# A GNN layer's node stage: another order of ScalarE's and TensorE's work within a step

## What is computed

```
h        = relu(layernorm(x))                             # every node
em       = relu(LN([h[src], h[dst]] @ msg_w + msg_b)) * edge_weight
messages = segment_mean(em, dst)                          # zero for a node without edges
gate     = sigmoid(h @ gate_w + gate_b)
h_new    = relu(LN([h, messages] @ upd_w + upd_b))
out      = x + gate * h_new + (1 - gate) * h
```

## Time and profile before

| | |
|---|---|
| median of 3 runs | 932.8 us |
| span of the profiled execution, first to last instruction | 994.9 us |
| granted TensorE clock, 100 to 500 us (node stage) | 0.50 |
| VectorE, ScalarE, TensorE busy over the span | 90%, 89%, 72% |
| mean granted TensorE clock over the span | 0.695 |

### The profile page before, as it was taken

How to read it: one execution, slowest core, us unless ns; L and a number is a source line. 1 busy time by engine, 2 the same in 40 slices (tenths; PEclk the granted TensorE clock), 3 DMA queues, 4 the chain that set the end, 5 groups by cost and what they waited for, 6 DMA issues and landing times.

```text
span 994.9 us, 19018 instructions
## 1 busy us (share of the span) xinstructions
PE 711.9 (72%) x3696; PEld 556.2 (56%) x3696; DVE 896.4 (90%) x3914; ACT 881.3 (89%) x3758; POOL 672.5 (68%) x602
## 2 busy tenths in 40 slices
PE   2477778777777777777756767787778787777861
PEld 1355556555555555555545656666656666666651
DVE  7499999999999999999997489999989999999984
ACT  3499999998999899989987689999999999999973
POOL 4677878777666667677757357677666776665466
PEclk9655555555555555555567789899889889998995
DMA  4244544455545555555423112233311211111110
GB/s 142 54 125 157 160 145 156 152 164 155 159 153 166 156 157 156 164 158 156 135 75 93 45 56 92 80 95 97 97 63 53 66 64 65 61 54 57 53 70 33
DMA packets 60147, 107.94 MB, mean 108 GB/s; under 512 B 14278, under 2 KB 16150, under 8 KB 60082
## 3 DMA queue, kind: packets, MB, share of 16 engines
q1 hardware_dynamic: 39756, 71.88, 20.8%
q0 software_dynamic: 18912, 34.84, 13.5%
q10 hardware_dynamic: 1414, 0.53, 0.2%
HBM read 56.01 MB, written 55.12 MB: 112 GB/s over the span
## 4 chain that ended last, share of the span: by engine, by line
ACT 60%; PE 13%; issue 11%; DVE 6%; another core or an unknown queue 6%; POOL 3%; ACTq 1%; DMA 1%; DVEq 0%; POOLq 0%
ACT hrow L392 16%; ACT junk L399 16%; ACT work L426 10%; ACT xload L392 4%; PE pt L1177 3%; ACT rs L379 3%; PE pm L1229 3%; ACT lnv L374 3%; POOL out L596 3%; PE pm L1231 3%; ACT work L1102 2%; PE py L1248 2%; ACT at L1045 2%; ACT work L1045 2%
## 5 line engine op out<-in xcount | busy, mean ns | idle before, releaser
L596 POOL DMA_INDIRECT out<-work,sidx x196 | 209.4, 1069 | 124.4 <-issue 55.6
L591 POOL DMA_INDIRECT ring<-in_x,src_i x196 | 220.0, 1123 | 90.5 <-issue 57.3
L1177 PE MATMUL pt<-ident,hrow 128*128 128x128 f32 x588 | 147.4, 399 | 142.6 <-ACT hrow L392 119.5
L426 ACT ACTIVATE work<-work,gt 128x128 f32<-128x128 f32 x589 | 205.1, 426 | 4.2 <-issue 3.0
L1211 PE MATMUL py<-w_u,work 128*128 128x129 f32 x784 | 204.5, 442 | 0.0
L1211 PEld LDWEIGHTS py<-w_u,work 128*128 128x128 f32 x784 | 175.6, 329 | 40.8 <-issue 40.8
L1177 PEld LDWEIGHTS pt<-ident,hrow 128*128 128x128 f32 x588 | 99.0, 202 | 175.6 <-ACT hrow L392 146.0
L591 POOL DMA_INDIRECT ring<-in_x,gidx x140 | 156.9, 1121 | 53.7 <-issue 42.2
L399 ACT ACTIVATE junk<-py 128x128 bf16<-128x128 f32 x588 | 155.4, 293 | 29.9 <-remote 29.8
L392 ACT ACTIVATE hrow<-xload,nb,rs 128x128 f32<-128x128 f32 x392 | 163.5, 514 | 3.0 <-DVE nb L385 2.7
L458 DVE SCALAR_TENSOR_TENSOR work<-py,rs,g_upd 128x128 f32<-128x128 f32 x588 | 163.2, 338 | 0.0
(11 more groups left out here) (163 smaller groups left out, 1506.7 us busy)
## 6 DMA issues: line engine op xcount, KB each, us to landing
xload<-in_x SPq DMA_DIRECT2D x98, 256.0 KB
out<-work SPq DMA_DIRECT2D x98, 256.0 KB
running_sums<-acc SPq DMA_DIRECT2D x49, 256.0 KB
staged_target_rows<-work SPq DMA_DIRECT2D x14, 256.0 KB
ring<-staged_target_rows SPq DMA_DIRECT2D x14, 256.0 KB
ring<-in_x,src_i POOLq DMA_INDIRECT x196
out<-work,sidx POOLq DMA_INDIRECT x196
ring<-in_x,gidx POOLq DMA_INDIRECT x140
```

The source lines that it names most:

```text
L426: last = nc.scalar.activation(t_buf[:, g.at % 4, k, :], t_buf[:, g.at % 4, k, :], ACT.Relu, scale=gt[:, g.at % 4, k:k + 1])
L591: pool.indirect_dma_start(out=dest, out_offset=None, in_=rows, in_offset=bass.IndirectOffsetOnAxis(ap=idx, axis=0), **(if_tail if rows is ...
L596: pool.indirect_dma_start(out=out, out_offset=bass.IndirectOffsetOnAxis(ap=idx, axis=0), in_=rows, in_offset=None, **if_tail).then_inc(s, 16)
L1177: last = nc.tensor.transpose(dest[:, k * H:(k + 1) * H], rows[:, k, :], ident[:, :])
```

## The change

ScalarE's step becomes: one gated row, logarithm, second gated row, reciprocal deviation, two gated rows, evacuation, four squares, gate exponential, four normalised rows. The special order of the first four steps goes. TensorE's step becomes: bias and product of group s-2, then the flip of group s-1. No instruction, wait, buffer or size is added or removed; a few register instructions of the loops aside, the same instructions stand in another order. The last six node steps run inside `edge_step`, whose ScalarE order stays, while TensorE's `node_step` is called there too and has the new order.

```diff
@@ ScalarE, node_step(s), after logs(act, nd, s, 2 * G)
-                filling = not beyond(s, 4)
-                if filling:
-                    rstds(act, nd, s, 2 * G)
+                if live(r, NG):
+                    gated_relu(act, nd, r, 2, first=1, done=False)
+                rstds(act, nd, s, 2 * G)
+                if live(r, NG):
+                    gated_relu(act, nd, r, first=2)
                 g = s.back(2)
                 if live(g, NG):
                     evacuate(nd, g, ht_dst[:, g.at % 4, :], pt[:, g.at % 2, :], ACT.Copy, "ht", "flip")
-                if not filling:
-                    rstds(act, nd, s, 2 * G)
-                if live(r, NG):
-                    gated_relu(act, nd, r, first=1)
+                node_post(s)
                 node_h(s)
-                node_post(s)
@@ TensorE, node_step(s)
-                g = s.back(1)
-                if live(g, NG):
-                    nd["h"].after(pe, g)
-                    one_mark(nd["flip"], pe, g, flip(pt[:, g.at % 2, :], hrow[:, g.at % 4]))
                 g = s.back(2)
                 if live(g, NG):
                     nd["ht"].after(pe, g)
...
                     one_mark(nd["upd"], pe, g, last)
+                g = s.back(1)
+                if live(g, NG):
+                    nd["h"].after(pe, g)
+                    one_mark(nd["flip"], pe, g, flip(pt[:, g.at % 2, :], hrow[:, g.at % 4]))
```

## The result

| | before | changed |
|---|---|---|
| median of 4 runs | 932.83 us | 937.85 us (937.23 to 939.3) |
| ratio, with its 95% interval | | 1.0055 (1.0041 to 1.0069) |
| span of a profiled execution | 994.9 us | 935.5 us, own time 937.23 us |

The changed kernel is slower by 5.0 us. It lies inside the range, on the side of the rival "the ring itself is the bound" (939 us).

What follows compares the result with a forecast made beforehand. The prediction took the node stage to be bound by VectorE at 4.60 us per step, ScalarE close behind at 4.52. All terms were taken as 0, so the forecast stayed at 933 us, range 921 to 948.

Steps and rivals of the forecast that it cites:

- no change: Node stage: VectorE keeps 4.60 us per step in both orders; 933 us, 931 to 935; chance 0.33.
- the ring itself is the bound: Node stage: bias matmuls wait for `gamma`, ScalarE for the flip in most steps; about +6, 939 us; chance 0.18.
- the ring: Two-step closed chain: `gamma`, product, flip, evacuation, squares, normalised rows, logarithm, reciprocal deviation, `gamma`; 4.56 to 4.65 us per step, term 0.
- Work, start and hand-over: All engines' work unchanged; start and last steps inside the edge stage move 0.5 to 1 us either way; term 0.
- Second gated row ahead of the reciprocal deviation: ScalarE: reciprocal deviation does not wait for the logarithm and comes 0.18 us earlier; VectorE has no gap there; term 0.
- Squares ahead of rows: ScalarE: gate exponential comes 1.54 us earlier, already hidden by VectorE's work; normalised rows later, `nb` long done; term 0.
- the floor: VectorE's own time per undisturbed node step, 4.60 us, claimed to stand unchanged; ScalarE's is 4.52.
- Late marks: TensorE's marks coming after the modelled end, making ScalarE wait; term taken as 0, between -23 and +21 us.
- more slack: ScalarE's squares: slack for late product marks grows from 0.68 to 1.22 us; -4 to -8, about 926 us; chance 0.22.
- The granted clock should stay at 0.50: TensorE, node stage: same work in an equally long step keeps 1.2 GHz; a rise would shorten the ring.
- The bound that the prediction named: Node stage: the forecast is wrong if undisturbed steps differ from 4.60 us by over 0.03.

Runs made afterwards that it cites:

- the second control: The kernel before, run again with no edit on a slower chip beside the changed kernel; ratio 0.9985 (0.9955 to 1.0016).
- logarithm first: The changed kernel with ScalarE's logarithm moved ahead of the first gated row; ratios to the kernel before 1.0042 and 1.0058 on two chips.
- one more gated row: The changed kernel with three gated rows instead of two ahead of the reciprocal deviation; ratio to the kernel before 1.0179 (1.0129 to 1.0230).
- the exchange: The changed kernel with the normalised rows put back ahead of the squares and gate exponential; ratio to the kernel before 1.0038 (1.0015 to 1.0060).

## Why the prediction was right or wrong

The range (921 to 948) held 937.85. The likeliest case, no change (931 to 935), was wrong: the kernel is slower by 0.55%. That the total fell so near the ring rival's 939 us is in part luck, since the ring gives 2.4 of the 5.0 us and that rival had no loss at the start.

1. *Work, start and hand-over, priced 0 ("0.5 to 1 us either way").* Work was right, for VectorE's and ScalarE's instructions cost the same. The hand-over too: the intervals that lead into the edge stage are 5.38, 7.57, 8.39 and 8.0 us in the changed kernel and 5.38, 7.57, 8.41 and 8.0 in the second control. **The start failed**: on the other chips the fifth gate comes about 3 us later, three times the bound given, of which 1.5 us are traced to the order. The step assumed that an evacuation or a flip shifts by one place; what mattered for the 1.5 us was that VectorE must first fall 2 us behind ScalarE before the new order flows. On the first chip the start was not measured in both orders. There the changed kernel's first five gates take 47.98 - 28.15 = 19.8 us for four intervals, 1.4 over 4 x 4.60, and the rest of the 5.0 us beside the ring is 2.6: that it is the start is argued from this and from the other chips, not shown. Nor is the edge stage ruled out: from the 98th gate to the end, four profiles of one chip take 465.8 us (kernel before), 468.7 (changed), 470.4 (logarithm first) and 463.9 (one more gated row), a scatter in which 2.6 us would not be seen.

2. *Second gated row ahead of the reciprocal deviation, 0.* Right in the sense that the reciprocal deviation never waits for the logarithm (209.91 + 0.31 = 210.22 against 210.39), but a gated row's 0.29 lies in the ring on either side of the logarithm, and this is what decides between 4.60 and 4.63.

3. *Squares ahead of rows, 0.* Right for steady steps together with TensorE's order (the exchange changed nothing), wrong in the start: the 1.5 us of item 1 are there with the squares ahead and gone with the rows ahead.

4. *The ring, 4.56 to 4.65 per step, taken at 4.56.* **This is the term that failed, by its size.** All its joints were where the prediction put them and all but one had their predicted length: 0.06, 0.54, 1.88 on TensorE, 4.07 for 4.06 on ScalarE, 1.62 for 1.61 on VectorE. The flip behind a product took 1.06, not 0.93. The 0.93 was read where the granted clock was on its way up: the products ahead of it took 0.64 us each and those behind it 0.39, and the stretch from 966 to 970 us has a granted clock of 0.73, while the node stage that it was applied to ran at 0.50. With 1.06 the sum is 9.24, or 4.62 per step, over the floor of 4.60, and the rival of the ring would have been the forecast, with 88 x 0.02 = 1.8 us; measured are 9.27 and 2.4 us. The rival's price, +6, came near the total for the wrong reason: it rested on engines that run faster without a profile, while the profiled execution of the changed kernel is one of its timed runs, at 937.23 us, and its floor is 4.60 too.

5. *Late marks, 0, between -23 and +21.* The term held as a sum and was wrong about its cause. They do not come from profiling, and go with the chip as far as is seen (each chip was measured at one time only): the same kernel takes 932.8, 975.3, 973.3 and 995.2 us on four chips, and in its profiles from two of the latter three undisturbed steps are 4.60 us. In the changed kernel's profile from the first comparison there are none, so that nothing was to be gained by slack in it. The rival "more slack" found no support on the chips with late marks either: what waits in the new order is the evacuation, and two events cost 3.1 and 3.2 us where one of the old order cost 1.2.

6. *"The granted clock should stay at 0.50".* Wrong: 0.63. The text said that a risen clock would shorten the ring and save the forecast. The clock rose only in part: product and flip ran 2.09 and 1.06 us long in the steps shown, and 1.16 and 0.79 in others (309.73 and 311.59), and only with the longer times does the ring bind: behind that fast flip the evacuation starts 0.49 us after its end, not 0.04.

The bound that the prediction named, undisturbed steps off 4.60 by more than 0.03, was nearly met by the mean (0.027) and exceeded by the 35 longer ones.

## What to carry to other kernels

When a reordering closes a new ring through two in-order engines, add it up for as many steps as it spans, with every duration from a stretch at the same clock, and compare it with the floor: here 0.13 us in one instruction decided, on a ring of 9.27 against a floor of 9.20. Then add up the rings that close within one step, for each half of the change too. And price the fill by itself: an order that needs one engine to lag behind the other can pay for that lag once, at the start (1.5 us here).

## What the runs showed of the hardware

- *The same work at another clock.* The control ran its node stage at a granted clock of 0.51, hence at 1.2 GHz nearly throughout, and the changed kernel at 0.62 and 0.63 on two chips, which is a mixture of 1.2 and 2.4 GHz, with less TensorE busy time (262.64 and 263.51 us of 400 against 313.87). The control and the changed kernel on the same chip:

```profile
100.00:500.00 400.00, 313.87 (x1205) 225.90 (x1205) 398.39 (x1891) 395.04 (x1719) 309.66 (x255) 0.51 0.52 159
```

```profile
100.00:500.00 400.00, 263.51 (x1185) 196.53 (x1184) 394.50 (x1862) 390.66 (x1688) 305.01 (x253) 0.62 0.51 158
```

 In the old order TensorE pauses 0.87 us ahead of the flip in each step; in the new one it pauses 1.1 us ahead of the bias matmuls. What of this lets the clock rise is open.

- *Late marks go with the chip.* On three chips out of four the engine that waits for a matmul's mark starts up to about 2 us after the modelled end (1.60 and 1.88 in the rows above), alone or two in a row, at places that differ from run to run, and later still in the first steps (a wait of 13.2 us); on the fourth, one profile shows none. Whether it is the chip or the time of the measurement, and what causes them, stays open.
